# A split-precision mixture-of-experts layer on one core: second-layer weights and batch 1's x turned in 32 by 32 blocks on VectorE, two batches' plan remade

## The reference, cut to what matters

```
nx       = layer_norm(x) * gamma + beta
weights  = softmax((nx @ Wq) @ (ctx @ Wk)^T / 16)       # 64 context rows of the batch
evidence = weights @ (ctx @ Wv)
combined = [nx, evidence, cond]                         # 768
p        = softmax(combined @ router_W + router_b)      # 3 experts
h_e      = silu(combined @ e_w1[e] + e_b1[e])           # 512 hidden, e = 0, 1, 2
routed   = sum_e p_e * (h_e @ e_w2[e] + e_b2[e])
g        = sigmoid(silu(combined @ gate_w1 + gate_b1) @ gate_w2 + gate_b2)
out      = x + g * (routed @ out_w + out_b)
```

## Time and profile before

| | us |
|---|---|
| median of 3 runs | 446.98 |
| lowest, highest | 446.29, 447.31 |
| profiled execution, its own time | 446.62 |
| its span from first to last instruction | 444.8 |
| PE busy | 434.5 |
| DVE busy | 308.8 |
| ACT busy | 246.5 |
| POOL busy | 92.4 |

### The profile page before, as it was taken

One profiled execution on the slowest core, in us unless ns is written; L12 is line 12 of the kernel. 1 busy time (PEld: TensorE's weight loads), 2 busy tenths in 40 slices (PEclk: granted clock), 3 DMA queues, 4 the chain that ended last, 5 costly groups with the idle time before them and its releaser, 6 DMA issues.

```text
span 444.8 us, 5728 instructions
## 1 busy us (share of the span) xinstructions
PE 434.5 (98%) x1934; PEld 349.9 (79%) x1934; DVE 308.8 (69%) x576; ACT 246.5 (55%) x383; POOL 92.4 (21%) x82
## 2 busy tenths in 40 slices
PE   8999999989999999999999999999999999999993
PEld 7578878868888878888788878888888878888882
DVE  2786747788877867786687867786587757663456
ACT  2346854746674747475474656564565556455430
POOL 1201000530233123132124032312024022402200
PEclk9999999999999999999999999999999999999998
DMA  8679257204375436543444425633542525133202
GB/s 230 159 210 280 92 185 150 47 19 124 87 177 155 113 87 142 131 107 96 94 96 143 92 75 120 171 70 93 116 105 64 141 58 112 25 86 81 47 0 47
DMA packets 73006, 49.26 MB, mean 111 GB/s; under 512 B 49322, under 2 KB 62418, under 8 KB 72978
## 3 DMA queue, kind: packets, MB, share of 16 engines
q1 hardware_dynamic: 71648, 48.35, 43.8%
q10 hardware_dynamic: 1218, 0.29, 0.3%
q0 software_dynamic: 112, 0.26, 0.2%
HBM read 26.77 MB, written 7.41 MB: 77 GB/s over the span
## 4 chain that ended last, share of the span: by engine, by line
PE 96%; DVE 2%; issue 0%; DVEq 0%; ACT 0%
PE bank L575 37%; PE bank L825 34%; PE bank L801 12%; PE bank L598 2%; PE bank L653 2%; PE bank L695 2%; PE bank L620 1%; PE bank L665 1%; PE bank L710 1%; DVE work L1267 1%; PE bank L641 1%; PE bank L725 1%; PE bank L586 0%; PE bank L607 0%; PE bank L703 0%
## 5 line engine op out<-in xcount | busy, mean ns | idle before, releaser
L575 PE MATMUL bank<-nx,w1n 128*128 128x512 f32 x672 | 173.8, 394 | 0.0
L1001 ACT ACTIVATE hf<-bank,zb 128x512 f32<-128x512 f32 x112 | 77.2, 689 | 130.2 <-PE bank L801 128.9
L825 PE MATMUL bank<-h,w 128*128 128x512 f32 x576 | 147.3, 392 | 1.5 <-DVE h L1337 1.5
L575 PEld LDWEIGHTS bank<-nx,w1n 128*128 128x128 f32 x672 | 125.9, 188 | 28.4 <-issue 1.0
L825 PEld LDWEIGHTS bank<-h,w 128*128 128x128 f32 x576 | 108.1, 188 | 26.8 <-DVE h L1337 2.0
L1337 DVE TENSOR_TENSOR h<-hf,h 128x512 fp32r<-128x512 f32 x112 | 86.0, 772 | 60.5 <-ACT h L1004 57.7
L1004 ACT ACTIVATE h<-bank,zb 128x512 fp32r<-128x512 f32 x112 | 76.5, 683 | 0.0
L801 PE MATMUL bank<-wT,vw 128*128 128x512 f32 x224 | 71.0, 398 | 0.0
L801 PEld LDWEIGHTS bank<-wT,vw 128*128 128x128 f32 x224 | 41.8, 188 | 9.5 <-DVE wT L1114 0.2
L1368 POOL TENSOR_TENSOR xq<-xq,quad 128x512 f32<-128x512 f32 x14 | 18.2, 1325 | 112.1 <-DVE quad L1073 112.1
L1383 POOL TENSOR_TENSOR work<-work 128x512 f32<-128x512 f32 x14 | 18.1, 1292 | 62.9 <-DVE work L1267 62.9
(11 more groups left out here) (140 smaller groups left out, 424.9 us busy)
## 6 DMA issues: line engine op xcount, KB each, us to landing
vw<-vw_pair SPq DMA_DIRECT2D x48, 256.0 KB, 3.7
xn<-in_x_dram SPq DMA_DIRECT2D x8, 512.0 KB, 4.4
p_bc<-prob_dram SPq DMA_DIRECT2D x8, 512.0 KB, 5.1
xq<-in_x_dram SPq DMA_DIRECT2D x32, 128.0 KB, 2.7
out_dram<-xq SPq DMA_DIRECT2D x28, 128.0 KB, 3.3
stage<-in_L_xcond_e_w_dram SPq DMA_DIRECT2D x6, 512.0 KB, 5.3
xhat_dram<-xn SPq DMA_DIRECT2D x6, 512.0 KB, 2.9
quad<-xhat_dram SPq DMA_DIRECT2D x24, 128.0 KB, 2.9
```

Source lines behind the costliest of these rows:

```text
L575: mm = pe.matmul(dst, lhs(a), rhs(c), start=first and i == 0, stop=last and i == n - 1)
L825: mm = pe.matmul(o, lhs, h[:, s % HRING, a, :], start=c == 0 and i == 0, stop=c == COUNT[g] - 1 and i == 2)
L1001: act.activation(hf[:, s % 2, :], z, ACT.Silu, bias=zb[:, j, b:b + 1]).then_inc(s_h, 1)
```

## The change

- `e_w2` is loaded into the stage in four partition groups (four transfers of 128 KB, 64 numbers a row, where there was one of 512 KB). DVE turns it by one 32 by 32 block transpose of 128x1024 (`ew_turn`). PE's 24 transposes and ACT's 6 copies are gone. The rows of `e_b2` and `out_w` are loaded in the matching order (one more small DMA on ACT; `out_w` by two DMAs on POOL, where it was one on SP).
- `TURN0` is 1: batch 1's x is normalised in place, stored to DRAM and loaded back, both issued by POOL, and turned by DVE. PE's 8 transposes of it are gone.
- The plans of batches 0 and 1 are remade: `b2` and its output leave the start-up, statistics and normalisation of batch 1 come at slots 3 and 4 (1 and 3 before), its turning at slot 7 and its parts at slot 8 (slot 4 before), scores in the middle of slot 9 (ahead of it before), `wg` after slot 11's own work (in its middle before), `vsplit0` and `vsplit4` in batch 1 (slots 10 and 13 of batch 0 before).
- `load_x(2)` on SP moves behind `store_p(0)`. ACT splits `gate_w2` ahead of `w_hi(0)`. A plus entry now puts ACT's step behind the slot's silu, for every batch.

```diff
-    TURN0 = 2
+    TURN0 = 1
+    FIRST_NORM = (3, 4)
-        B2_BANK = 3
+        B2_BANK = 6
...
-        FIRST_PLAN = {2: ["ewT0", "rm_"], 3: ["fold0", "shi2"], 4: ["px_", "zb2+", "xT+", "slo2+", "pr_"],
-                      5: ["ewT1"], 6: ["fold1", "split3"], 7: ["vwp3", "ewT2+", "vsplit1"], 8: ["fold2", "vsplit3"],
-                      9: ["zb3", "sc", "vsplit2"], 10: ["vsplit0"], 11: ["ex", "wg+"], 12: ["whi", "vr", "wlo"], 13: ["vsplit4"]}
-        SECOND_PLAN = {1: ["lg_"], 4: ["px_", "nx", "pr_+"], 6: ["vwp0", "sc+"], 7: ["vwp1+"], 8: ["wg"], 9: ["ex", "vwp2+"],
+        FIRST_PLAN = {0: ["b2o", "ewT0"], 2: ["b2+", "rm_"], 3: ["fold0", "shi2"], 4: ["px_", "zb2+", "slo2+", "ewT1+"],
+                      5: ["pr_"], 6: ["fold1", "split3", "ewT2"], 7: ["xt", "vwp3"], 8: ["fold2", "nx", "vsplit1"],
+                      9: ["sc+", "zb3", "vsplit3"], 10: ["vsplit2"], 11: ["ex", "wg"], 12: ["whi+", "vr+"], 13: ["wlo+"]}
+        SECOND_PLAN = {1: ["lg_", "vsplit0"], 3: ["vsplit4"], 4: ["px_", "nx", "pr_+"], 6: ["vwp0", "sc+"], 7: ["vwp1+"], 8: ["wg"], 9: ["ex", "vwp2+"],
...
+                else:
+                    early, late = ("post", "post") if inner and engine == "act" else \
+                        ("mid", "mid") if inner else ("pre", "post")
...
+        def turn_x(eng, b):
+
+            eng.wait_ge(s_xhat, b + 1)
+            if b > TURN0:
+                eng.wait_ge(*x_turned(b - 1))
+            written, turned = (s_x1w, s_x1r) if b == TURN0 else (s_xhw, s_xhr)
+            eng.dma_start(xhat_dram.rearrange("(t p) h -> p t h", p=PART), xn[:, :, :]).then_inc(written, 16)
...
+            eng.wait_ge(*x_written(b))
+            for q in range(QUADS):
+                eng.dma_start(quad_of(quad, q), quad_view(xhat_dram, q)).then_inc(turned, 16)
...
                 if kind == "w2":
                     dst = stage[:, u % STAGES, :, :].rearrange("p k n -> p (k n)").rearrange(
-                        "p (i h) -> p i h", h=H)
-                    src = e_w2[g].rearrange("(i p) h -> p i h", p=PART)
...
+                        "p (j c) -> p j c", c=H // QUADS)
+                    for q in range(QUADS):
+                        sp.dma_start(quad_of(dst, q), quad_view(e_w2[g], q)).then_inc(s_stage[u % STAGES], 16)
...
-            load_x(2)
             load_staged("n", 3)
             load_staged("c", 3)
             load_staged("w2", 2)
             store_p(0)
+            load_x(2)
             load_p(0)
...
-            def w2_transpose(e):
...
-            def ew_copy(e):
...
+            def ew_turn(e):
+                i, arrived = stage_of("w2", e)
+                dve.wait_ge(*arrived)
+                if e >= 1:
+                    dve.wait_ge(s_fold, 2 * e)
+                raw = stage[:, i, :, :].rearrange("p k n -> p (k n)").rearrange("p (j k b) -> p k j b", k=KC, b=QROWS)
+                dve.transpose(ewT.rearrange("p k (j a) -> p k j a", a=QROWS), raw).then_inc(s_ewT, 1)
...
-            pool.wait_ge(s_ow, 16)
+            pool.wait_ge(s_prep, PREP["vT1"])
+            for k in range(KC):
+                pool.dma_start(ow_in[:, k, :], quad_rows(out_w)[k]).then_inc(s_ow, 16)
+            pool.wait_ge(s_ow, 16 * KC)
...
             reciprocal_std(1)
+            turn_x(pool, 1)
```

More of the change, by code:

```diff
@@ L310, in plan @@
                     steps += [(name, *args)] if when == ("mid" if inner else "pre") and name in PE_STEPS else []
-                elif when == "pre":
-                    steps += [(f, *args) for f in pre.get(engine, [])]
-                elif when == ("mid" if inner and engine == "dve" else "post"):
-                    steps += [(f, *args) for f in post.get(engine, [])]
+                else:
+                    early, late = ("post", "post") if inner and engine == "act" else \
+                        ("mid", "mid") if inner else ("pre", "post")
+                    steps += [(f, *args) for f in pre.get(engine, []) if when == early]
+                    steps += [(f, *args) for f in post.get(engine, []) if when == late]
             if when == "post" and engine == "act" and j == GB + LAG - 1:
```

106 lines of the change are left out of this document (47 added, 59 removed).

## The result

| | before | after |
|---|---|---|
| median of 4 runs each, same chip | 446.63 | 452.95 |
| lowest, highest | 446.12, 447.31 | 452.40, 455.23 |
| profiled execution | 446.62 | 452.4 |
| its span | 444.8 | 450.6 |
| granted clock over the span | 0.996 | 0.983 |

The ratio is 1.015, with an interval of 1.0112 to 1.0188. I had forecast 444.0 in a range of 442.0 to 446.5. The change made the kernel slower by 6.3 us where I expected 3 us of gain, and the time lies outside the range.

What follows compares the result with a forecast made beforehand. PE, busy for 434.5 of 444.8 us, was taken as the bound. The terms -3.2 - 1.5 + 1.0 + 0.2 + 0.1 + 0.1 + 0.3 = -3.0 took the median from 446.98 to 444.0, range 442.0 to 446.5.

Steps and rivals of the forecast that it cites:

- PE's transposes, -3.2: Three weights and batch 1's x: four groups of transposes leave PE, 0.79 us each, minus 3.2 us.
- The low part of slot 11 and wT, -1.5 and +1.0: Slot 11's low part, now ahead of the softmax steps, loses its 1.5 us wait; wT then comes 1.0 us late.
- ACT's plus entries, which I costed at 0: Later positions of ACT's plus entries put silu ahead of a cast, where nothing waited before: 0 us.
- One more issue on ACT at the start ... 0 to 0.35, I take 0.1: At the start, one more DMA issue of 0.35 us ahead of ACT's first copy: plus 0.1 us.
- Batch 1's x through DRAM: nothing: Batch 1's x, stored and reloaded by POOL, lands by 63 to 66.7, before the limit of 69 us: no cost.
- "nothing" for the load of the router probabilities: This load, behind x(2) on SP, must wait for its own store until 59 anyway: no cost.
- The first value load, +0.1 (bounds 0 and 1): The first four-part weight load, 64 numbers a row, stands ahead of the first value load: plus 0.1 us.
- DVE's turns, +0.2: Four turns of 1.24 us on DVE in batch 0; only the first lacks room, at fold 0: plus 0.2 us.
- Batch 1's splits, +0.3: Two splits moved from batch 0 to batch 1 on DVE, with ACT's casts: plus 0.3 us, bounds 0 and 1.6.
- The third: Rival: batch 1's x comes late through POOL's queue, scores wait at slot 9, time 450.9; chance 0.07.
- The fourth rival: VectorE is the wrong place: DVE limits slots 0 to 8, its 5.0 us of turns all show, 448.8; chance 0.05.
- all is hidden: Rival: wT is in time and the small terms are zero, minus 4.7 us, 442.3; chance 0.15.

Runs made afterwards that it cites:

- e11: The kernel before with only `wg`, batch 1's softmax steps, moved behind slot 11's own low part; 449.17, ratio 1.0052.
- e13: The changed kernel with the last anchor product moved from slot 9 to slot 10; 452.35, ratio 1.012.
- e1: The changed kernel with the two issues of `e_b2`'s rows given to POOL instead of ACT; 452.81, ratio 1.0136.
- e12: The changed kernel with batch 1's x turned by PE again and `e_b2`'s rows issued by POOL; 446.12, ratio 0.9994.
- e15: e12 with batch 1's scores in slot 8, softmax steps behind slot 10, and the second weight turn first in slot 4; 446.09, ratio 0.9989.
- e8: e5 with `e_b2`'s rows issued by POOL and the first `w2` load behind the first value loads; 447.47, ratio 1.002.
- e10: e9 with `e_b2`'s rows issued by POOL and the first `w2` load behind the first value loads; 447.48, ratio 1.0033.
- e3: The changed kernel with SP's `load_x(2)` behind the loads of the router probabilities, not ahead of them; 452.02, ratio 1.0112.
- e5: The changed kernel with batch 1's x stored and loaded by SP instead of POOL, and x(2) behind those loads; 447.54, ratio 1.0023.
- e9: The changed kernel with batch 1's x turned by PE at slot 4 again, without the trip through DRAM; 447.57, ratio 1.0027.
- e16: The kernel before with batch 1's scores in slot 8, softmax steps behind slot 10, and `vsplit0` moved from slot 10 to 11; 449.88, ratio 1.0071.
- e14: e5 with `e_b2`'s rows issued by POOL and the last anchor product in slot 10; 447.14, ratio 1.0012.
- e6: The changed kernel with DVE's turn of batch 1's x behind the low parts of the third fold, not ahead; 452.46, ratio 1.014.

## Why the prediction was wrong, by its own steps

**PE's transposes, -3.2: right.** 32 records are gone. By the starts of the four pieces it is 3.2 us; from the first evidence product to the third fold it is 3.8 (32.1 us where it took 35.9), of which 0.3 lie in the first evidence piece.

**The low part of slot 11 and wT, -1.5 and +1.0: right in this kernel,** to the place. The tenth (1.05) is partly luck: the low part of slot 11 took 1.14 us and ended about 0.8 later against PE than I reckoned, and the steps behind it took 4.1 us and not 4.8. And the working had the gain as a property of `wg`'s place; e11 shows that this move alone loses 2.8 us, and its trace points at ACT's plus entries, which I costed at 0.

**"One more issue on ACT at the start ... 0 to 0.35, I take 0.1": failed.** It measured 2.9. I took the duration of the old issue for the new ones, which are two, of another shape, at 0.8 us each. And I took PE's wait as its whole price, without the clock (1.3 of the 2.9). The upper bound of 0.35 was the old issue's own time, and so no bound for another shape.

**"Batch 1's x through DRAM: nothing" and "nothing" for the load of the router probabilities: failed.** 2.9 us of wait and 3.3 of clock. Two things went wrong in it. I asked when the scores need x, but PE's next need of DVE was the anchor product's bank behind `fold_lo(2)`, a user of what is queued behind the turn. That alone is not decisive: with the bank taken away (e13) the wait is 3.5 us at the scores. And I costed each transfer by the nearest row of another crowd, the probabilities only by their issue time (one us late), and not by what would run beside them. The store was written at 61.5 and not by 57.5, the last quad came at 72.3 (out at 63.5, 8.8 to landing) and not at 63 to 66.7, and `p_bc` at 71.1 and not near 63.6: 9.1 us instead of 4.2. Data by 69 us was the limit I gave. The chain also began 3.4 us later than I had it, since PE did (normalised at 55.4, not 52.0), but that is not the cause: in e1, with the start-up mended, PE's wait is 3.8.

**The first value load, +0.1 (bounds 0 and 1): mis-sized,** 0.8. e12, e15 and e1 still show 0.5 to 1.1 of it, and e13 1.5. e8 and e10, with the first `w2` load behind the value loads, list no such wait, so it is that load, ahead of the value loads, that makes it; in e10 a wait came up at the anchor product's stage instead. Whether its 64-number rows or its place count, and what POOL's two for `out_w` do, was not tried apart.

**DVE's turns, +0.2: right while PE is late.** No fold waited in the changed kernel. With PE in time they show: 1.3 us at the second fold in e12, and 0 when that turn is put first in slot 4 (e15). **Batch 1's splits, +0.3: 0,** no wait there.

**The rivals.** The third, at 0.07, had the late x right, and the wait near slot 9. Its size and its path were not these: the quads took 10.8 us from the first issue to the last landing, where it had 18.4 and the prediction's bounds were 5.2 and 9.2; and DVE stood for `p_bc` first, which it did not name. Only in e3, with `p_bc` mended, does DVE wait for the quads alone (3.1 us). That they go out on POOL's queue is not shown to be the reason. The fourth rival (VectorE the wrong place) is not borne out: e5 removes the loss without moving a turn. That all is hidden, or the sum of 444.0, was reached by no version: most of what was taken from PE came back as a wait at the next link that had that much room. PE at 98% busy had hidden how near they all were.

**Which pieces are bad.** The trip of batch 1's x through DRAM as it was queued, with `p_bc` behind x(2), about 5.4 us, by e5 and by e9; the rows of `e_b2` on ACT about 1.4 by e9 against e12, and nothing while slot 9 waits, by e1. The turned weights with the plan (e12): no measurable difference.

## What to carry to other kernels

When work is taken from an engine that never waits, list for each other engine the next thing it is needed for, and by how much it is ahead; the gain is bounded by these leads, not by the work removed. When an instruction waits longer, ask who is queued behind it and which buffer they hold, not only who wants its own result. Cost a DMA issue by its own shape: a rearranged row can have a different price from the same bytes in one piece. And cost a load in a crowd by what is queued ahead of it and beside it: the same bytes landed in 3.3 or 10.5 us by their place.

## What the runs showed of the hardware

- **A wait of TensorE can cost more than itself.** Behind 2.08 us at 8.14 and 2.86 at 76.66 the granted clock stood at 0.50 for some us, for 1.3 and 3.3 us of time. So it did behind 1.92 in e16, 2.22 in e9, 2.39 in e14, 2.8 in e3, 3.5 in e13 and 3.8 in e1. But behind 1.5 to 1.8 us at the first place it stayed at 1.00 in e3, e5, e6 and e13, behind 1.52 in the kernel before, and behind 3.0 in e11 too.
- **The issue of one small transfer on ACT can cost over twice that of its neighbour.** The two of `e_b2` (three rows in four pieces of 32 numbers) took 0.72 and 0.85 us; the others there, among them those of `ln_gamma` and `ln_beta` (two rows in four such pieces), took 0.28 to 0.54. What in the shape makes the difference was not tried.
- **In a crowd of transfers the order decides who lands late.** `p_bc`, 512 KB, landed in 9.1 to 10.3 us with x(2) ahead of it and the four quads on POOL beside it, in 5.6 with x(2) behind it and the quads still on POOL, in 5.5 with the quads on SP and x(2) behind, and in 4.4 to 4.5 without the quads. x(2) landed in 3.3 us when it went first, in 7.9 when it went last (e5), and in 10.5 when it went out among the quads and landed last (e3). Whether the queue matters besides is open.
- **VectorE's two-input instructions of 0.69 us took 1.6 to 1.8 while GpSimd ran its products** (e16), so the same steps cost by their place. Not each one pays so: before, a low part took 1.01 there, and a transpose kept its 0.68 while GpSimd's product took 1.79 instead of 1.29.
